# Routed expert outputs weighted at PSUM and added into two sums in DRAM, with all gate and up weights on chip

## The chip, the cores and the metric

The kernel runs on one core of a Trainium2 chip. Times are device microseconds of one launch, in timed runs without a profile. The kernel before was timed three times; its median is 205.45 us.

## What is computed

Eight sequences of 128 tokens with 256 channels (1024 tokens, float32) go through two blocks. The first is a WKV recurrence over time, with keys from the layer norm of `x` and values from the context, and its result is added to `x`. The second is a mixture of experts: 32 experts, 4 picked for each token, no more than 256 rows kept for one expert. Cut to what matters:

```python
x = x + wkv(time_decay, time_first, layernorm(x), ctx)            # 8 x 128 x 256
h = rmsnorm(layernorm(x)) * norm_w
scores = softmax(h @ gate_w.T); topk_w, topk_ids = top_k(scores, 4); topk_w /= sum(topk_w)
buf[expert, pos] = h[token]                                       # E=32 experts, C=256 rows each
g, u = split(buf @ w13)                                           # w13: 32 x 256 x 256
eo = (silu(g) * u) @ w2                                           # w2:  32 x 128 x 256
routed[token] += eo[expert, pos] * topk_w                         # 4096 picks in all
out = x + layernorm(x) + routed + shared_expert(h)
```

## The kernel before

The work is written by hand for each engine: every engine has its own program, and semaphores order them. SP (SyncE) issues nearly all plain DMAs, POOL issues all indirect ones. A queue issues in the order of its program, so what stands behind a waiting instruction waits too. The kernel has three stages.

**Routing stage** (the `run([...])` lists). Eight sequences pass through a software pipeline on PE, DVE, ACT and POOL. For each sequence `b` it ends with the picks of 128 tokens: `slot_all[:, b, k]` is the row of the DRAM table `rows_in` (32 experts, `ROWS_E` = 1024 rows each) into which pick `k` of a token goes. `n_row[:, b, :]` is the normalised token with 8 tag columns behind it (the four expert numbers, then the four numbers of the picks), which ACT copies from `tags` (L459). POOL issues four indirect DMAs a sequence (`scatter`, L318), 32 in all, each writing 128 rows of 264 floats. Meanwhile SP issues (L192 to L227) the inputs, 32 DMAs of zeros into the first 256 rows of every expert in `rows_in` (L204; unused rows must be zero), the weights `w13` of the first four experts (L210) and all of `w2` (L227, four DMAs of 1 MB). At the end DVE adds the shared expert's output to `base_all` (L682).

**Expert stage.** For expert `e` SP loads its 256 rows into one of `WB` = 4 buffers `xg` (L214). PE transposes them (`rows_to_channels`, L874), ACT copies them from PSUM to SBUF (L476), PE multiplies with gate and up weights (`gate_up_half`, L882), ACT takes silu (L481), DVE multiplies (L730), PE multiplies with `w2` (`down_half`, L899), DVE copies the 256 output rows from PSUM into `yo` (L737). The second half of the 256 rows is computed only where an expert has over 128 rows (`pe.If`). POOL scatters the output with two indirect DMAs of 128 rows each into `rows_out` (`scatter_out`, L333), a DRAM table with one row for each of the 4096 picks. Where a row goes is worked out by DVE from the tags (L718, L722, L724); unused rows get a number outside the table and are left out. PE's order is transposes of `e + 1`, gate and up of `e`, down of `e - 1`. `w13` of later experts is loaded four experts ahead (L210). `yo`, `xg`, `w13b` and `pick_idx` all have four buffers, so DVE waits for the scatter of expert `e - 4` (`row_out`) before it works out the rows of expert `e`. SP also stores the last output row of every expert (`store_last`, L221) for an overflow case that this data doesn't take. On ACT, DVE, POOL and SP the middle experts run in a loop of four experts an iteration (`Fori`).

**Last stage.** SP waits for all scatters, loads the four picks of every token (`G`, nine DMAs, 4 MB, L265), and DVE (five sequences, L769) or ACT and POOL (three sequences, L503 and L372) weight them with `w_all` and add them to `base_all`. Eight DMAs write the result.

The scatter that the change touches:

```python
def scatter_out(e, q):
    pool.wait_ge(s["pick_ready"], e + 1)
    pool.wait_ge(s["f_yo"], e + 1)
    for a in range(2):
        pool.indirect_dma_start(rows_out, bass.IndirectOffsetOnAxis(ap=pick_idx[:, q, a:a + 1], axis=0),
                                yo[:, q, a, :], None, bounds_check=PICKS - 1, oob_is_err=False)\
            .then_inc(row_out[q], 16)
```

Of the kernel before, what the change touches and what calls it, by code (L numbers as in the profile page):

```python
# [4 lines left out]
F32 = mybir.dt.float32  # L5
BF16 = mybir.dt.bfloat16
I32 = mybir.dt.int32
# [5 lines left out]
P = 128  # L13
# [7 lines left out]
PICKS = B * T * K  # L21
RW = C + 2 * K
OUTSIDE = 16384
U_MAX = 60.0
POOL_SUMS = (1, 3, 6)
FIRST = 2
W2L = 4
SHARED_AFTER = 5
WB = 4


def xattn_moe(nc, x, ctx_in, time_decay, time_first, norm_w, gate_w, w13, w2, sh_gate, sh_up, sh_down, out):
    ctx = ExitStack()
    with ctx:
# [3 lines left out]
        def sem(name):  # L38
# [4 lines left out]
        rows_out = nc.dram_tensor("rows_out", (PICKS, C), F32, kind="Internal").ap()  # L43
# [6 lines left out]
        w_all = sb("w_all", [P, B, K])  # L50
        slot_all = sb("slot_all", [P, B, K], I32)
        tags = sb("tags", [P, B, 2 * K])
# [4 lines left out]
        big = sb("big", [P, E], I32)  # L57
# [24 lines left out]
        zeros = sb("zeros", [P, 4 * RW])  # L82
# [32 lines left out]
        ew = sb("ew", [P, B, K])  # L115
        esum = sb("esum", [P, B])
        rsum = sb("rsum", [P, B])
# [5 lines left out]
        late_row = sb("late_row", [P, C])  # L123

        w13b = [sb(f"w13b{q}", [P, HC, 2, F]) for q in range(WB)]
        w2_all = sb("w2_all", [P, E, C])
        xg = [sb(f"xg{q}", [P, 2, RW]) for q in range(WB)]
        own = sb("own", [P, WB, 2, K])
        owned = sb("owned", [P, WB, 2])
        pick_idx = sb("pick_idx", [P, WB, 2], I32)  # L130
        xT = sb("xT", [P, 2, HC, CAP])
        sg = sb("sg", [P, 2, CAP])
        act_t = sb("act_t", [P, 2, CAP])
        sg_all = sb("sg_all", [P, B, T])
        yo = sb("yo", [P, WB, 2, C])
        G = sb("G", [P, B, K, C])
        res = sb("res", [P, B, C])
        part = sb("part", [P, 2, K - 1, C])
        pool_part = sb("pool_part", [P, K - 1, C])
# [15 lines left out]
        names = """held_pool colT_ready cols6_done x0_in x1_in v0_in v1_in col_in gw_in sh_in sdn_in zero_set consts ident_set tri_set  # L155
# [3 lines left out]
            top_ready idx_done expert_ready nmax_done ew_ready rsum_done w_done tagged onehot_done mask_ready  # L159
            pos_ready slots_done picked_done slot_ready own_done owned_done pick_ready fits_done last_all_done last_set slot_max_done slot_top_done overflow_done fixed pickno_ready  # L160
            gu_ready gu_done sh_s sh_a tot_ready big_done beyond_done sh_y sh_b f_xt f_x f_g f_s f_a f_y f_yo tail_part res_ready weighted pool_part_done pool_res_ready""".split()
        s = {n: sem(n) for n in names}
        scattered = [sem(f"scattered{b}") for b in range(B)]
        w_in = [sem(f"w_in{q}") for q in range(WB)]
        w2_in = [sem(f"w2_in{g}") for g in range(W2L)]
        xg_in = [sem(f"xg_in{q}") for q in range(WB)]
        row_out = [sem(f"row_out{q}") for q in range(WB)]
        gathered = [sem(f"gathered{b}") for b in range(B + 1)]
        last_stored = [sem(f"last_stored{q}") for q in range(WB)]
# [4 lines left out]
        pool_out_done = sem("pool_out_done")  # L174
# [13 lines left out]
        def _(sp):  # L188
# [10 lines left out]

            sp.wait_ge(s["zero_set"], 1)  # L200
            zv = rows_in.rearrange("(e n) c -> n e c", n=ROWS_E)
            for a in range(2):
                for e in range(0, E, 2):
                    sp.dma_start(zv[a * P:(a + 1) * P, e:e + 2, :],  # L204
                                 zeros[:, 0:2 * RW].rearrange("p (e c) -> p e c", e=2)).then_inc(zeroed[a], 16)

            sp.dma_start(sdn[:, :], sh_down).then_inc(s["sdn_in"], 16)

            def load_weights(e, q):
                sp.dma_start(w13b[q][:, :, :, :].rearrange("p h a f -> p h (a f)"),  # L210
                             w13[bass.ds(e, 1)].rearrange("o (h p) f -> p (o h) f", p=P)).then_inc(w_in[q], 16)

            def load_rows(e, q):
                sp.dma_start(xg[q][:, :, :],  # L214
                             rows_in[bass.ds(e * ROWS_E, CAP), :].rearrange("(a p) c -> p a c", p=P))\
                    .then_inc(xg_in[q], 16)

            def store_last(e, q):

                sp.wait_ge(s["f_yo"], e + 1)  # L220
                sp.dma_start(last_rows[bass.ds(e, 1), :], yo[P - 1:P, q, 1, :]).then_inc(last_stored[q], 16)  # L221
# [725 lines left out]
```

## Time and profile before

| | us |
|---|---|
| timed runs, median of 3 | 205.45 |
| timed runs, lowest and highest | 204.16 to 205.67 |
| span of the one profiled execution | 228.0 |
| busy in that span: PE, DVE, POOL, ACT | 139.5, 120.4, 115.6, 84.8 |
| chain that ended last, largest shares | PE 36%, issue 20%, SP queue 19% |

The profile is one execution, which took longer than the timed ones. The page gives busy times of each engine, the span in 40 slices of 5.7 us (busy tenths, the TensorE clock in tenths, GB/s of the DMA engines), and groups of instructions by source line. The chain of waits goes back from the last instruction, at each step to what released it. The timeline lists instructions in order of time, with the idle time before each one in brackets.

### The profile page before, as it was taken

The page shows a single profiled execution, that of the slowest core. Times are in us where ns is not written, and L with a number is a line of the kernel's source. Part 1 is how long each engine was busy: PE and PEld are TensorE (multiplying, and loading weights), DVE is VectorE, ACT ScalarE, POOL GpSimd, SP SyncE. Part 2 cuts the span into 40 slices and gives each one's busy share as a digit, 9 for nine tenths or more (in the row PEclk, how much of TensorE's full clock was granted, in tenths as well). Part 3 has the DMA queues.
Part 4 walks back from the last instruction along what each step waited for, and adds up shares of the span by engine and source line. Part 5 has one row for each costly group of instructions (what it writes and reads, how often), then busy time and mean ns, then how long its engine had stood idle before and what let it go on. Part 6 is the DMA issues. An engine that isn't in the chain of part 4 may idle for free.

```text
span 228.0 us, 3659 instructions
## 1 busy us (share of the span) xinstructions
PE 139.5 (61%) x819; PEld 119.8 (53%) x819; DVE 120.4 (53%) x385; ACT 84.8 (37%) x254; POOL 115.6 (51%) x140
## 2 busy tenths in 40 slices
PE   1124887787774879969895948858499479200000
PEld 0112765676663559959794837837398377100000
DVE  2878999997433344555253531536237055303990
ACT  3165678566563024434214231335225032002410
POOL 6201156888877500754563736555464646632740
PEclk9999996555555799988999788999979958755555
DMA  5999999998222264775775657465665731129930
GB/s 173 334 340 340 338 339 364 365 373 301 96 99 95 95 198 134 235 204 153 218 198 176 192 161 220 136 189 158 185 172 171 232 115 52 43 69 359 385 122 23
DMA packets 40270, 46.46 MB, mean 204 GB/s; under 512 B 4585, under 2 KB 37045, under 8 KB 40252
## 3 DMA queue, kind: packets, MB, share of 16 engines
q1 hardware_dynamic: 35200, 37.30, 53.2%
q0 software_dynamic: 4608, 8.54, 10.5%
q10 hardware_dynamic: 444, 0.40, 0.5%
q8 instruction: 9, 0.15, 0.2%
q14 instruction: 9, 0.07, 0.1%
HBM read 27.95 MB, written 22.45 MB: 221 GB/s over the span
## 4 chain that ended last, share of the span: by engine, by line
PE 36%; issue 20%; SPq 19%; another core or an unknown queue 7%; DVE 7%; DMA 5%; ACT 2%; POOL 0%; POOLq 0%; ACTq 0%; DVEq 0%
PE bank L882 18%; PE bank L899 11%; SPq L204 10%; PE bank L874 8%; SPq L227 5%; DVE part L769 4%; DMA G<-rows_out 3%; DVE act_t L730 1%; ACT xT L476 1%; DMA xg<-rows_in 1%; ACT sg L481 1%; DVE res L769 1%; SPq L210 1%; DMA rows_out<-yo,pick_idx 1%
## 5 line engine op out<-in xcount | busy, mean ns | idle before, releaser
L333 POOL DMA_INDIRECT rows_out<-yo,pick_idx x64 | 62.6, 978 | 55.7 <-issue 47.8
L882 PE MATMUL bank<-xT,w13b 128*128 128x128 f32 x368 | 51.6, 294 | 8.5 <-issue 5.6
L882 PEld LDWEIGHTS bank<-xT,w13b 128*128 128x128 f32 x368 | 48.1, 208 | 11.0 <-issue 11.0
L476 ACT ACTIVATE xT<-bank,cols 128x256 f32<-128x256 f32 x64 | 26.8, 473 | 43.0 <-PE bank L874 37.0
L899 PE MATMUL bank<-w_all,act_t 128*128 128x256 f32 x92 | 29.7, 434 | 16.0 <-DVE act_t L730 14.9
L730 DVE TENSOR_TENSOR act_t<-sg,bank 128x256 f32<-128x256 f32 x32 | 13.5, 421 | 49.3 <-ACT sg L481 36.5
L318 POOL DMA_INDIRECT rows_in<-n_row,slot_all x32 | 32.5, 1015 | 10.0 <-issue 10.0
L481 ACT ACTIVATE sg<-bank 128x256 f32<-128x256 f32 x32 | 12.3, 386 | 44.6 <-PE bank L882 25.1
L899 PEld LDWEIGHTS bank<-w_all,act_t 128*128 128x128 f32 x92 | 16.5, 209 | 18.8 <-issue 17.9
L737 DVE COPY yo<-bank 128x512 f32<-128x512 f32 x32 | 22.0, 687 | 6.6 <-remote 3.3
L874 PE MATMUL bank<-ident,xg 128*128 128x128 f32 x128 | 22.0, 301 | 1.3 <-DMA xg<-rows_in 1.2
L874 PEld LDWEIGHTS bank<-ident,xg 128*128 128x128 f32 x128 | 18.0, 157 | 6.2 <-issue 2.7
L839 PE MATMUL bank<-hT,sgu 128*128 128x128 f32 x64 | 16.1, 432 | 0.0
L308 POOL TENSOR_TENSOR rs<-ve,neg_half 128x2 f32<-128x2 f32 x8 | 5.9, 736 | 17.4 <-DVE ve L624 17.3
L839 PEld LDWEIGHTS bank<-hT,sgu 128*128 128x128 f32 x64 | 14.3, 326 | 0.0
L503 ACT ACTIVATE G<-G,w_all 128x256 f32<-128x256 f32 x12 | 5.1, 496 | 17.1 <-DMA G<-rows_out 17.1
L810 PE MATMUL bank<-ident,n_row 128*128 128x128 f32 x16 | 5.3, 430 | 9.6 <-ACT n_row L431 9.6
L718 DVE SCALAR_TENSOR_TENSOR own<-xg,iota_e 128x8 f32<-128x8 f32 x32 | 7.0, 219 | 7.4 <-issue 4.4
L562 DVE TENSOR_TENSOR_SCAN S<-decay,bank 128x512 f32<-128x512 f32 x8 | 9.7, 1209 | 1.1 <-PE bank L794 1.1
L769 DVE SCALAR_TENSOR_TENSOR part<-G,w_all,base_all 128x256 f32<-128x256 f32 x5 | 3.8, 767 | 10.4 <-DMA G<-rows_out 10.4
L794 PE MATMUL bank<-ident,ek 128*128 128x128 f32 x16 | 5.1, 420 | 6.4 <-DVE ekv L556 6.3
L819 PE MATMUL bank<-gwT,hT 128*128 128x32 f32 x32 | 7.5, 374 | 1.8 <-ACT hT L444 1.8
(109 smaller groups left out, 194.3 us busy)
## 6 DMA issues: line engine op xcount, KB each, us to landing
rows_in<-zeros SPq DMA_DIRECT2D x32, 264.0 KB, 6.4
xg<-rows_in SPq DMA_DIRECT2D x32, 264.0 KB
w13b<-in_L_ffn_w_dram SPq DMA_DIRECT2D x32, 256.0 KB
w_all<-in_L_ffn_w_dram SPq DMA_DIRECT2D x4, 1024.0 KB
G<-rows_out SPq DMA_DIRECT2D x7, 512.0 KB, 7.1
rows_out<-yo,pick_idx POOLq DMA_INDIRECT x64
x_all<-in_x_dram SPq DMA_DIRECT2D x1, 768.0 KB, 5.2
v_all<-in_ctx_dram SPq DMA_DIRECT2D x1, 768.0 KB, 7.6
```

Source lines behind the costliest of these rows:

```text
L204: sp.dma_start(zv[a * P:(a + 1) * P, e:e + 2, :], zeros[:, 0:2 * RW].rearrange("p (e c) -> p e c", e=2)).then_inc(zeroed[a], 16)
L318: pool.indirect_dma_start(rows_in, bass.IndirectOffsetOnAxis(ap=slot_all[:, b, k:k + 1], axis=0), n_row[:, b, :], None)\
L333: pool.indirect_dma_start(rows_out, bass.IndirectOffsetOnAxis(ap=pick_idx[:, q, a:a + 1], axis=0), yo[:, q, a, :], None, bounds_check=PICK ...
L476: act.activation(xT[:, j, h, :], FX[j][:, h, :], ACT.Copy, scale=nw[:, h:h + 1]).then_inc(s["f_x"], 1)
L481: act.activation(sg[:, j, :], FG[j][:, 0, :], ACT.Silu).then_inc(s["f_s"], 1)
L730: dve.tensor_tensor(act_t[:, j, :], sg[:, j, :], FG[j][:, 1, :], ALU.mult).then_inc(s["f_a"], 1)
L737: dve.tensor_copy(yo[:, q, :, :], FY[q % 2]).then_inc(s["f_yo"], 1)
L769: dve.scalar_tensor_tensor(out=dst, in0=G[:, b, k, :], scalar=w_all[:, b, k:k + 1], in1=src, op0=ALU.mult, op1=ALU.add)\
L839: last = nc.tensor.matmul(SGU[:, a, :], sgu[:, h, a, :], hT[:, j, h, :], start=(h == 0), stop=(h == HC - 1))
L874: last = nc.tensor.transpose(FX[q % 2][:, h, a * P:(a + 1) * P], xg[q][:, a, h * P:(h + 1) * P], ident[:, :])
L882: last = nc.tensor.matmul(FG[q % 2][:, a, cols], w13b[q][:, h, a, :], xT[:, q % 2, h, cols], start=(h == 0), stop=(h == HC - 1))
L899: return nc.tensor.matmul(FY[q % 2][:, a, :], act_t[:, q % 2, a * P:(a + 1) * P], w2_all[:, bass.ds(e, 1), :].rearrange("p o c -> p (o c)" ...
```

## The change

It does these things together:

- **Weights.** All of `w13` gets its place in SBUF (`w13_all`, 64 KB a partition). SP loads it in eight DMAs of 1 MB between the four of `w2`, all ahead of the first row load. The loads of 256 KB within the expert stage are gone. `yo[e]` lies over `w13` of the same expert, once that is used, so each expert has its own output buffer.
- **Sums.** `rows_out` is replaced by `sums`: two tables of 1280 rows (256 spare rows, then the 1024 tokens). The tokens of the first table start as `base_all` (a store of 1 MB that SP issues after the first six row loads), the second table and the spare rows as zeros (1.5 MB, issued behind the weights). Expert `e` adds to table `e % 2`.
- **Scatter.** `scatter_out` uses `compute_op=ALU.add`: the DMA reads the rows in DRAM, adds, and writes them. Unused rows are added to the spare rows, so all 128 rows of each DMA are moved. As two additions to one row must not overlap, POOL waits for expert `e - 2` to have landed before it issues the scatter of `e`. The wait for `pick_ready` is gone.
- **Weighting.** A row of `rows_in` is two floats longer (266): expert numbers, the four exponentials, one over their sum, and the row in `sums`. DVE writes the expert numbers straight into `n_row`, ACT the exponentials, and DVE the reciprocal (`pick_norm`). DVE weights the output as it copies it from PSUM (two `tensor_scalar` of 256 columns instead of one copy of 512).
- **Order and buffers.** No `Fori` is left on any engine. `xg` has six buffers. DVE works out rows two experts ahead. Gate and up matmuls take 256 columns at once instead of 128 twice. The flags `second` are bits of two registers loaded once, instead of a load for each expert. ACT copies the last output rows (`last_to_sbuf`), and one DMA stores them all.
- **Last stage.** SP loads the two sums (eight DMAs, 2 MB), DVE adds them (four additions), and four DMAs write the result.

The core of the diff:

```diff
-            for q in range(WB):
-                load_weights(q, q)
+            for g in range(EARLY):
+                load_w13(g)
+                if g % 2 == 0:
+                    load_w2(g // 2)
+            sp.dma_start(sums[0:SPARE].rearrange("(p a) c -> p (a c)", a=2), zero_rows).then_inc(sums_zeroed, 16)
+            sp.dma_start(sums[ACC:2 * ACC].rearrange("(p n a) c -> p n (a c)", p=P, a=2),
+                         zero_rows.unsqueeze(1).to_broadcast([P, ACC // (2 * P), 2 * C])).then_inc(sums_zeroed, 16)
...
             for b in range(B):
                 sp.wait_ge(scattered[b], 16 * K)
+            for e in range(XB):
+                load_rows(e)
+            sp.wait_ge(s["sh_b"], B // 2)
+            sp.dma_start(sums[SPARE:ACC].rearrange("(b p) c -> p b c", p=P), base_all[:, :, :]).then_inc(base_stored, 16)
...
             def scatter_out(e, q):
-                pool.wait_ge(s["pick_ready"], e + 1)
                 pool.wait_ge(s["f_yo"], e + 1)
-                pool.sem_inc(s["held_pool"], 1)
+                if e >= ACCS:
+                    pool.wait_ge(row_out[(e - ACCS) % YB], 32 * ((e - ACCS) // YB + 1))
                 for a in range(2):
-                    pool.indirect_dma_start(rows_out, bass.IndirectOffsetOnAxis(ap=pick_idx[:, q, a:a + 1], axis=0),
-                                            yo[:, q, a, :], None, bounds_check=PICKS - 1, oob_is_err=False)\
-                        .then_inc(row_out[q], 16)
+                    pool.indirect_dma_start(sums, bass.IndirectOffsetOnAxis(ap=pick_idx[:, e, a:a + 1], axis=0),
+                                            yo[e][:, a, :], None, compute_op=ALU.add).then_inc(row_out[q], 16)
...
-                dve.tensor_copy(yo[:, q, :, :], FY[q % 2]).then_inc(s["f_yo"], 1)
+                for a in range(2):
+                    last = dve.tensor_scalar(yo[e][:, a, :], FY[e % 2][:, a, :], owned[:, e, a:a + 1],
+                                             xg[e % XB][:, a, NORM:NORM + 1], ALU.mult, ALU.mult)
+                last.then_inc(s["f_yo"], 1)
...
+            for c in range(B // 2):
+                dve.wait_ge(sum_in[c], 16 * ACCS)
+                dve.tensor_tensor(G[0][:, 2 * c:2 * c + 2, :], G[0][:, 2 * c:2 * c + 2, :], G[1][:, 2 * c:2 * c + 2, :],
+                                  ALU.add).then_inc(s["res_ready"], 1)
...
                 with pe.If(second != 0):
-                    for a in range(2):
-                        gate_up_half(q, a, slice(P, 2 * P))
-                for a in range(2):
-                    last = gate_up_half(q, a, slice(0, P))
-                last.then_inc(s["f_g"], 1)
+                    gate_up_slots(e, j, CAP)
+                with pe.Else():
+                    gate_up_slots(e, j, P)
```

## Rows read from the trace of the kernel before

**Rows 1.** The page: share of the chain, and the 40 slices for clock and DMA.

```profile
PE 36%; issue 20%; SPq 19%; another core or an unknown queue 7%; DVE 7%; DMA 5%; ACT 2%; POOL 0%; POOLq 0%; ACTq 0%; DVEq 0%
PEclk9999996555555799988999788999979958755555
GB/s 173 334 340 340 338 339 364 365 373 301 96 99 95 95 198 134 235 204 153 218 198 176 192 161 220 136 189 158 185 172 171 232 115 52 43 69 359 385 122 23
```

**Rows 2.** Stretches of time: busy us of each engine (instructions), clock, DMA share, GB/s.

```profile
32.00:54.00 22.00, 15.94 (x85) 13.27 (x83) 20.83 (x80) 16.38 (x63) 17.17 (x18) 0.59 1.08 366
54.00:79.00 25.00, 17.18 (x85) 14.13 (x86) 10.61 (x39) 9.63 (x32) 18.60 (x20) 0.54 0.32 116
98.00:198.00 100.00, 75.77 (x474) 66.39 (x474) 42.16 (x137) 30.43 (x79) 53.93 (x56) 0.89 0.57 167
```

**Rows 3.** The page's groups for indirect DMAs and expert matmuls.

```profile
L333 POOL DMA_INDIRECT rows_out<-yo,pick_idx x64 | 62.6, 978 | 55.7 <-issue 47.8
L882 PE MATMUL bank<-xT,w13b 128*128 128x128 f32 x368 | 51.6, 294 | 8.5 <-issue 5.6
L318 POOL DMA_INDIRECT rows_in<-n_row,slot_all x32 | 32.5, 1015 | 10.0 <-issue 10.0
```

**Rows 4.** Timeline of the expert stage: first output copy, then scatters on POOL.

```profile
89.04 0.69 DVE L737 COPY yo<-bank 128x512 f32<-128x512 f32 x1
90.64 1.20 POOL L333 DMA_INDIRECT rows_out<-yo,pick_idx  x1 [6.95 <-DVE pick_idx L724]
...
117.05 0.98 POOL L333 DMA_INDIRECT rows_out<-yo,pick_idx  x1 [0.31 <-issue]
118.33 0.98 POOL L333 DMA_INDIRECT rows_out<-yo,pick_idx  x1 [0.30 <-issue]
120.28 0.97 POOL L333 DMA_INDIRECT rows_out<-yo,pick_idx  x1 [0.97 <-issue]
121.56 0.97 POOL L333 DMA_INDIRECT rows_out<-yo,pick_idx  x1 [0.30 <-issue]
```

**Rows 5.** Timeline of PE over the first experts, outside any loop.

```profile
88.84 0.60 PE L874 MATMUL bank<-ident,xg 128*128 128x128 f32 x4
91.93 0.60 PE L874 MATMUL bank<-ident,xg 128*128 128x128 f32 x4
...
94.12 0.60 PE L874 MATMUL bank<-ident,xg 128*128 128x128 f32 x4
95.89 0.60 PE L874 MATMUL bank<-ident,xg 128*128 128x128 f32 x4
```

**Rows 6.** Chain of waits, pieces in order of time: start us, us, what.

```profile
79.17 2.78 DMA xg<-rows_in
82.08 0.64 PE bank L874 x4
...
86.35 1.79 PE bank L882 x16
88.14 0.87 PE bank L899 x4
...
176.79 5.72 another core or an unknown queue
...
200.99 2.30 DMA rows_out<-yo,pick_idx
203.44 0.35 SPq L265
...
222.11 0.48 DVE res L769
```

**Rows 7.** Timeline of the routing stage: first and last scatter, a sum of 512 columns.

```profile
31.48 1.31 POOL L318 DMA_INDIRECT rows_in<-n_row,slot_all  x1 [0.28 <-issue]
...
75.19 0.69 DVE L682 TENSOR_TENSOR base_all<-base_all,bank 128x512 f32<-128x512 f32 x1 [1.25 <-issue]
76.65 0.96 POOL L318 DMA_INDIRECT rows_in<-n_row,slot_all  x1 [0.30 <-issue]
```

**Rows 8.** Timeline of the last stage: the first gathered sequence is there.

```profile
206.78 0.48 DVE L769 SCALAR_TENSOR_TENSOR part<-G,w_all,base_all 128x256 f32<-128x256 f32 x1 [8.58 <-DMA G<-rows_out]
```

More of the change, by code:

```diff
@@ new lines, in _ @@
+            for e in range(E):
+                if e + XB < E:
+                    sp.wait_ge(s["f_xt"], e + 1)
+                    sp.wait_ge(s["f_yo"], e + 1)
+                    load_rows(e + XB)
+                if e % 2 == 0 and EARLY + e // 2 < W13L:
+                    load_w13(EARLY + e // 2)
+                    if (EARLY + e // 2) % 2 == 0:
+                        load_w2((EARLY + e // 2) // 2)
+            sp.wait_ge(s["f_raw"], E)
+            sp.dma_start(last_rows.rearrange("(o e) c -> o e c", o=1), w2_all[P - 1:P, :, :]).then_inc(last_stored, 16)
@@ L677, in _ @@
             dve.wait_ge(s["tot_ready"], 1)
-            dve.tensor_scalar(big[:, :], TOT, CAP / 2 + 0.5, None, ALU.is_gt).then_inc(s["big_done"], 1)
+            dve.wait_ge(s["bit_set"], 5)
+            dve.scalar_tensor_tensor(out=halves[:, :], in0=TOT, scalar=CAP / 2 + 0.5, in1=bit[:, :], op0=ALU.is_gt,
+                                     op1=ALU.mult).then_inc(s["halves_done"], 1)
+            dve.wait_ge(s["halves_done"], 1)
+            with nc.allow_low_precision("sums of different powers of two below 2^16"):
+                dve.tensor_reduce(big[:, :], halves[:, :].rearrange("p (g n) -> p g n", n=BITS), AX.X, ALU.add)\
+                    .then_inc(s["big_done"], 1)
             for c in range(B // 2):
@@ L753, in _ @@
-            rows_out_to_sbuf(E - 1, WB - 1, E // WB - 1)
-            dve.wait_ge(s["sh_b"], B // 2)
-            dve.wait_ge(s["w_done"], 1)
-            mine = [b for b in range(B) if b not in POOL_SUMS]
-            for n, b in enumerate(mine):
-                dve.wait_ge(gathered[b], 16)
-                for k in range(K):
-                    src = base_all[:, b, :] if k == 0 else part[:, n % 2, k - 1, :]
-                    dst = res[:, b, :] if k == K - 1 else part[:, n % 2, k, :]
-                    if k:
-                        dve.wait_ge(s["tail_part"], (K - 1) * n + k)
-                    if b == B - 1 and k == K // 2:
-                        dve.wait_ge(gathered[B], 16)
-                    dve.scalar_tensor_tensor(out=dst, in0=G[:, b, k, :], scalar=w_all[:, b, k:k + 1], in1=src,
-                                             op0=ALU.mult, op1=ALU.add)\
-                        .then_inc(s["res_ready" if k == K - 1 else "tail_part"], 1)
+                    rows_out_to_sbuf(e - 1)
@@ L903, in down @@
+            def down(e, j, second):
+                if e % (E // W2L) == 0:
+                    pe.wait_ge(w2_in[e // (E // W2L)], 16)
                 pe.wait_ge(s["f_a"], e + 1)
[L904 to L905 removed]
                 with pe.If(second != 0):
[L907 to L911 removed]
```

353 lines of the change are left out of this document (156 added, 197 removed).

## The prediction

> **What bounds the kernel now.** I read the page first, then the chain of waits, then the timeline at each seam of the three stages. The chain's shares [rows 1] name PE (36%) and "issue" (20%), but an average over stages can't say what a change is worth, so I cut the span where the chain passes from one stage to the next [rows 6]: the first row load is released at 79.17 and PE starts on it at 82.08; the last scatter lands at 200.99 + 2.30 = 203.29; the last DVE sum ends at 222.59; the span ends at 228.0.
>
> The profiled span is 22.5 us above the timed median of 205.45. Part of that can be seen. The chain holds 7% (some 16 us) of "another core or an unknown queue" [rows 1], in pieces of up to 5.72 us in the middle of the expert stage, on a kernel with one core [rows 6]. I take these stalls, and the half clock that follows them, as belonging to the profiled execution. So I build a sum for the expert stage that doesn't hold them, and test it on the median.
>
> Two engines could pace that stage. **PE**: outside the loops it runs without a gap. One expert with over 128 rows takes 91.93 - 88.84 = 3.09 us, one with fewer 95.89 - 94.12 = 1.77 us [rows 5]. The 368 gate and up records [rows 3] are 8 for each of 32 experts and 8 more for each large one, so (368 - 256) / 8 = 14 are large. 14 x 3.09 + 18 x 1.77 = 75.1 us. **POOL**: one scatter takes 0.98 us and the next starts 0.30 us later, 1.28 us in all, so 2.56 us an expert; at a loop's end the gap is 0.97 instead of 0.30 [rows 4]. 32 x 2.56 = 82 us, and 8 loop ends at 0.67 add 5.4. So POOL needs more than PE, and with four buffers DVE and PE are held to it.
>
> The sum for before: first PE work 82.1; first scatter at 90.64, 8.6 later; 31 further experts at 2.56 make 79.4; seven loop ends 4.7; second scatter and landing 1.28 + 2.30 = 3.6; last stage 228.0 - 203.3 = 24.7. That is 203.1, 2.4 below the median. The sum holds well enough to go on: POOL's instruction rate, not PE, sets the expert stage in timed runs.
>
> **The change part by part.**
>
> *Weights and zeros ahead of the expert stage.* DMA is full (366 GB/s, share 1.08) to the slice that ends at 57 us, where it is 301 GB/s, then 96 [rows 1, 2]; I put the end of the queue at 55.5. Added to it: 28 x 256 KB of `w13` (7.34 MB), zeroing 1.57 MB, and 0.07 MB for longer zero rows, together 8.98 MB. The 32 scatters of the routing stage go on to 78.7 at 116 GB/s (2.7 MB from 55.5) [rows 2, 7]. (8.98 + 2.7) MB at 366 GB/s is 32 us, so the queue is empty at about 87.5. The row loads stand behind the weights in the same queue. Before, 2.9 us lie between the release and PE's start [rows 6]; now the load is issued before the queue is empty, so I add only 0.5 us: PE starts at 88.0, +5.9. Bounds: 0, if the weights got through beside the scatters, and +9 with the whole 2.9 behind 88. The routing stage itself stays as long: POOL is nearly without a gap from 31.48 to 77.6 [rows 7] and gets no DMA more; ACT's copy of tags goes, a reciprocal on DVE comes.
>
> *`base_all` store.* 1.05 MB behind six row loads (1.6 MB): 2.7 / 0.366 = 7.3 us after 87.5, so 95 and some landing time, against a first scatter at 88.0 + 8.6 = 96.6. Hidden by about 1 us; if not, it costs that.
>
> *Loops unrolled, flags loaded once, larger matmuls.* POOL loses its loop ends: -4.7. Matmuls of 256 columns take 0.87 / 4 = 0.217 us each, of 128 columns 1.79 / 16 = 0.112 [rows 6]: 8 of the one equal 16 of the other, so PE gains nothing here. DVE's second instruction at the output costs 0.3 us an expert on an engine busy 42 of 100 us [rows 2]; ACT's copy of the last rows is as small. Both lie beside POOL's pace. Without that cover they would have 2.35 us of PE an expert above them still.
>
> *No weight loads in the stage.* They lie beside POOL's work; nothing gained on the path. The scatter reads as well as writes now, and moves all 256 rows instead of 128 on average. Per expert 272 KB of rows, 262 KB read, 262 KB written: even if all three count, 0.8 MB at 366 GB/s is 2.2 us. Below POOL's pace, but no longer far below (167 GB/s before [rows 2]).
>
> *The new wait.* It stands on POOL, with all later scatters behind it, and for these only the last stage waits: every expert has its own output buffer, so PE and DVE run ahead. One table's cycle takes two experts: scatter, second scatter 1.28 later, landing 2.30 after its start [rows 6], plus x for the addition, plus the time from a semaphore to the start of the scatter, 90.64 - 89.73 = 0.9 us [rows 4]. Together 4.5 + x, against 2 x 2.56 = 5.12 of POOL's own. The wait is free up to x = 0.6; beyond, every us of x costs 15.5 us over the stage and 1 us at its end.
>
> The trace shows no accumulating DMA, so x is bounded. From below 0: nothing makes an addition land sooner than a plain write. From above a whole second transfer, 2.78 us like the row load [rows 6]. Between them: the first gathered sequence (512 KB) is used 206.78 - 203.44 = 3.34 us after its issue [rows 6, 8], of which 1.43 are bytes at 366 GB/s and 1.9 fixed for issue, read trip and receipt. The accumulating scatter already pays issue and receipt. A third of 1.9 for the read trip and 131 KB / 366 GB/s = 0.36 for the bytes give x = 1.0, which I take. The cycle is then 5.5, 2.75 an expert.
>
> That an addition reads as much again is also what the Trainium skill says ("Collectives: The Full Stack", "The bandwidth ceiling"): it needs two source reads. No row here shows it.
>
> *Is the instruction itself longer?* The two kinds of indirect DMA in the trace take 0.98 and 1.02 us in spite of different rows and targets [rows 3], so I take the same; with half as much again (0.5) it would be 64 x 0.5 = 32 us, less what the wait already costs (6): +26.
>
> *Last stage.* 2.1 MB instead of 4.2: 1.9 fixed + 5.7 of bytes + 0.1 to the first issue = 7.7. The last of four sums, 0.69 [rows 7]. From the last DVE end to the end of the span 228.0 - 222.6 = 5.4 as before, and 0.3 for an output DMA twice as large. Together 14.1 against 24.7: -10.6.
>
> **The sum.** 88.0 + 8.6 + 31 x 2.75 (85.3) + 1.28 + 2.30 + 1.0 + 14.1 = 200.6. The same sum for before was 2.4 too low, for waits between PE and POOL that a compute side running ahead mostly removes; I add 0.9: **201.5 us**, against 205.45.
>
> **The rivals.**
>
> *The wait is free* (x up to 0.6). Then 31 x 2.56 and x = 0.6: 88.0 + 8.6 + 79.4 + 4.2 + 14.1 + 0.9 = 195. For it: 1 KB rows are moved by 16 engines that stand at 57% in the stage [rows 2]. Against: now they must read first.
>
> *Landing decides, the other way* (slower). The place is the new wait. From x = 1.4 on the gain of the last stage is used up: 201.5 + 16.5 x 0.4 = 208. At x = 2 it is 218, at 2.78 it is 231. For it: under load a landing may be longer than the 2.30 read in a quiet moment at the end, and the row loads now share the engines with twice the scatter bytes. Against: the engines aren't full.
>
> The Trainium skill speaks for this one ("DMA: Bandwidth & Descriptors", "Latency and other measured facts"): HBM access takes 0.2 us on average and 2 us at high load. With an added read at the loaded figure x would be over 2 and the time about 220; with the other it would be the free wait. The trace has no row for a read under load within a scatter.
>
> *The instruction is longer*: 201.5 + 26 = 227, as above. Against it: both forms cost the same today.
>
> *The weights don't delay the start*, or the change there does nothing: 196 with x = 1.0. For it: reads of weights and writes of zeros may overlap better than the 366 GB/s. Against: DMA share 1.08.
>
> **How the numbers follow.** Forecast (x from 0.6 to 1.2, or 1.0 with the start where it was) 0.40; free wait 0.20; landing decides 0.30, of which a quarter within 1%; longer instruction 0.10. About 1% is what a measurement of this kernel can tell from no change: under 203.4 is faster, over 207.5 slower. The forecast's own range, 195 to 206, holds a sixth within 1%. So faster 0.33 + 0.20 = 0.53, same 0.07 + 0.07 = 0.14, slower 0.33. The range goes from 191 (free wait and an early start) to 222 (x = 2.2); above it are the rest of the landing rival and most of the longer instruction, about 1 in 8.
>
> **What would show it.** In the profile after: scatters on POOL about 2.75 us apart by expert, with gaps that end with a DMA landing; PE finished well before the last scatter; PE's first expert work near 88 with 366 GB/s up to there; the last stage near 14 us. Scatters 2.56 apart with gaps of 0.30 mean the free wait; pairs with gaps of over 1.5 us mean that landing decides; a mean above 1.2 us for the scatter means the instruction. If PE instead ends last, the reading that POOL sets the pace is wrong, and if the timed median differs from this sum while its steps are right, the stalls that I left out are in timed runs too.

## The result, and the profile after

| | before | after |
|---|---|---|
| timed, median of 4 runs (us) | 204.81 | 250.19 |
| lowest to highest | 203.62 to 205.67 | 248.59 to 251.89 |
| span of the profiled execution | 228.0 | 246.9 |

The kernel after takes 1.221 times as long as the kernel before, 95% interval 1.210 to 1.231. The prediction was 201.5 us, faster.

One thing about the measure itself comes out of the experiments and is needed to read them: beside the later kernels, on five other occasions, the kernel before took 232 to 237 us, while the kernel after, run again on one of them, took 249.2, nearly as at first. There the ratio is 1.058 (1.048 to 1.069). Each kernel below is compared with the runs of before that stand beside it. Where runs of one kernel lie apart, medians are of those within 1.5% of its fastest, while the expectations quote medians of all runs (222.3, 211.8, 238). Ratios with an interval are estimates over the same runs, and can differ from the ratio of two medians by half a per cent.

The page of after: the groups of the two indirect DMAs and of the weighting, then the 40 slices of 6.2 us. They answer to [rows 1, 3].

```profile
L342 POOL DMA_INDIRECT sums<-w_all,pick_idx x64 | 99.4, 1553 | 33.2 <-issue 16.6
L327 POOL DMA_INDIRECT rows_in<-n_row,slot_all x32 | 32.0, 1001 | 16.4 <-issue 15.5
L723 DVE TENSOR_SCALAR w_all<-bank,owned,xg 128x256 f32<-128x256 f32 x64 | 31.7, 537 | 0.6 <-PE bank L865 0.4
...
PEclk9999999955555569599999999999985555555555
GB/s 182 311 236 229 242 234 229 239 307 374 391 393 391 390 394 293 287 149 140 194 188 160 174 173 205 179 207 174 102 83 65 70 78 65 71 78 65 65 237 273
```

The adding scatter takes 1.55 us of POOL, the plain one took 0.98 [rows 3]. And from 12 to 49 us the DMA engines move 230 to 240 GB/s where the kernel before had 340 to 370 [rows 1]. The timeline of POOL in after shows where time goes at the start and in the expert stage, against [rows 4, 7]:

```profile
2.09 0.10 POOL L285 MEMSET var_add<- 128x1 f32 x1
11.31 0.16 POOL L286 IOTA iota_e<- 128x32 f32 x1 [9.12 <-issue]
...
54.02 1.11 POOL L327 DMA_INDIRECT rows_in<-n_row,slot_all  x1 [7.47 <-issue]
...
91.72 0.96 POOL L327 DMA_INDIRECT rows_in<-n_row,slot_all  x1 [0.30 <-issue]
98.69 0.38 POOL L335 PARTITION_ALL_REDUCE slot_top<-slot_max  x1 [6.01 <-issue]
110.81 1.80 POOL L342 DMA_INDIRECT sums<-w_all,pick_idx  x1 [11.73 <-DVE w_all L723]
...
114.76 1.55 POOL L342 DMA_INDIRECT sums<-w_all,pick_idx  x1 [0.30 <-issue]
116.61 1.54 POOL L342 DMA_INDIRECT sums<-w_all,pick_idx  x1 [0.30 <-issue]
119.55 1.54 POOL L342 DMA_INDIRECT sums<-w_all,pick_idx  x1 [1.39 <-DMA sums<-w_all,pick_idx]
...
230.15 1.55 POOL L342 DMA_INDIRECT sums<-w_all,pick_idx  x1 [0.30 <-issue]
```

POOL sits idle for 9 us before its first iota (an instruction that fills a tile with counted-up numbers). The routing scatters of the second sequence start at 54.0, and the last routing scatter at 91.7 instead of 76.7 [rows 7]. Then 64 adding scatters go out from 110.8 to 230.2, nearly always 0.30 us apart. The chain of waits in after at the two ends of the expert stage (start us, us, what), against [rows 6]:

```profile
91.72 5.87 DMA rows_in<-n_row,slot_all
...
97.67 2.81 DMA xg<-rows_in
...
100.53 1.13 PE bank L842 x4
...
230.15 3.61 DMA sums<-w_all,pick_idx
...
237.40 6.16 DMA v_all<-sums
243.58 0.69 DVE x_all L740
```

| step of the sum | predicted | after | difference |
|---|---|---|---|
| PE's first expert work | 88.0 | 100.53 | +12.5 |
| from there to the first scatter | 8.6 | 10.28 | +1.7 |
| first to last scatter (31 x 2.75 + 1.28) | 86.5 | 119.34 | +32.8 |
| last landing | 3.30 | 3.61 | +0.3 |
| last stage | 14.1 | 13.1 | -1.0 |
| allowance | 0.9 | - | -0.9 |
| span | 201.5 | 246.9 | +45.4 |

### The profile page after: what moved, and what is told of

Its sections match the earlier page's. It is cut to its first block, busy times and chain, and to the rows that moved or that the text cites. A ratio compares the mean times of both kernels' runs of the same rounds, so it can differ in the third digit from the quotient of the medians.

```text
span 246.9 us, 2751 instructions
## 1 busy us (share of the span) xinstructions
PE 126.7 (51%) x707; PEld 108.9 (44%) x707; DVE 115.3 (47%) x409; ACT 92.5 (37%) x266; POOL 144.1 (58%) x134
## 4 chain that ended last, share of the span: by engine, by line
PE 25%; DMA 22%; POOL 19%; SPq 16%; issue 14%; DVE 1%; POOLq 1%; ACT 1%; ACTq 0%
PE bank L851 14%; SPq L223 13%; DMA sums<-w_all,pick_idx 10%; POOL rows_in L327 9%; POOL sums L342 8%; PE bank L865 6%; PE bank L842 5%; DMA rows_in<-xT 4%; DMA xg<-rows_in 3%; DMA v_all<-sums 2%; DMA rows_in<-n_row,slot_all 2%; SPq L267 1%; POOL rs L316 1%; DVE w_all L723 1%; POOLq L41 1%
## 5 line engine op out<-in xcount | busy, mean ns | idle before, releaser
L342 POOL DMA_INDIRECT sums<-w_all,pick_idx x64 | 99.4, 1553 | 33.2 <-issue 16.6
L851 PE MATMUL bank<-xT,w_all 128*128 128x128 f32 (+1 forms) x256 | 46.6, 326 | 0.5 <-ACT xT L472 0.5
L851 PEld LDWEIGHTS bank<-xT,w_all 128*128 128x128 f32 x256 | 38.4, 194 | 3.4 <-issue 0.9
L723 DVE TENSOR_SCALAR w_all<-bank,owned,xg 128x256 f32<-128x256 f32 x64 | 31.7, 537 | 0.6 <-PE bank L865 0.4
L740 DVE TENSOR_TENSOR x_all<-x_all,v_all 128x512 f32<-128x512 f32 x4 | 2.8, 692 | 59.1 <-DMA v_all<-sums 59.1
L865 PE MATMUL bank<-w_all,act_t 128*128 128x256 f32 x92 | 25.7, 386 | 1.6 <-DVE act_t L717 1.3
L842 PE MATMUL bank<-ident,xg 128*128 128x128 f32 x128 | 20.1, 283 | 6.5 <-DMA xg<-rows_in 6.4
L842 PEld LDWEIGHTS bank<-ident,xg 128*128 128x128 f32 x128 | 16.3, 146 | 10.8 <-DMA xg<-rows_in 8.1
L482 ACT ACTIVATE w_all<-bank 32x256 f32<-32x256 f32 x32 | 12.1, 377 | 10.5 <-DVE w_all L723 9.8
L780 PEld LDWEIGHTS bank<-ident,n_row 128*128 128x128 f32 x16 | 2.2, 196 | 17.8 <-ACT n_row L432 17.8
## 6 DMA issues: line engine op xcount, KB each, us to landing
sums<-xT SPq DMA_DIRECT2D x1, 1280.0 KB, 11.5
```

The source lines that it names most:

```text
L342: pool.indirect_dma_start(sums, bass.IndirectOffsetOnAxis(ap=pick_idx[:, e, a:a + 1], axis=0), yo[e][:, a, :], None, compute_op=ALU.add).t ...
L482: act.activation(raw[e][P - 32:P, :], FY[e % 2][P - 32:P, 1, :], ACT.Copy).then_inc(s["f_raw"], 1)
L723: last = dve.tensor_scalar(yo[e][:, a, :], FY[e % 2][:, a, :], owned[:, e, a:a + 1], xg[e % XB][:, a, NORM:NORM + 1], ALU.mult, ALU.mult)
L842: last = nc.tensor.transpose(FX[j][:, h, a * P:(a + 1) * P], xg[e % XB][:, a, h * P:(h + 1) * P], ident[:, :])
L851: last = nc.tensor.matmul(FG[j][:, a, 0:slots], w13_all[:, e, h, a, :], xT[:, j, h, 0:slots], start=(h == 0), stop=(h == HC - 1))
L865: return nc.tensor.matmul(FY[j][:, a, :], act_t[:, j, a * P:(a + 1) * P], w2_all[:, e, :], start=True, stop=True)
```

## The experiments

### The row length and the adding form, one at a time

`a_rows272` is after with rows of 1088 bytes instead of 1064, the extra floats zero. `a_plain` is after with plain writes:

```diff
-RW = C + 2 * K + 2
+RW = 272
```
```diff
-                        yo[e][:, a, :], None, compute_op=ALU.add).then_inc(row_out[q], 16)
+                        yo[e][:, a, :], None).then_inc(row_out[q], 16)
```

> The changed kernel with rows of 272 floats (1088 bytes) instead of 266 (1064 bytes) in rows_in; six of them are zeros that nothing reads. Theory 'odd row length': DMA moves rows of 1064 bytes at 230 to 240 GB/s and rows of 1088 bytes at the 338 GB/s that 1056 bytes had before, so the zeros are done near 39 us instead of 54, and the first expert matmul starts near 88 instead of 100.5; the time falls by 10 to 14 us, to 236 to 240. Rival 'more bytes, late POOL': the start is late because of 9 MB more in the queue and of POOL's late first instructions; then 250 stays (2% more bytes, +1 us) and GB/s in the first 50 us stays below 250.

> The changed kernel with plain writes instead of additions in the 64 scatters to sums (the sums are left out, only the last writer stays); all waits stay. Theory 'the instruction': an accumulating DMA_INDIRECT keeps POOL for 1.55 us, a plain one for 0.98, so the pace falls from 1.85 to 1.28 us a scatter and the time by 63 x 0.57 = 36 us, to about 214. Rival 'landing': the wait for the scatter two experts back paces the stage; then gaps before the scatters stay over 0.3 us and the fall is what landing loses (3.7 to 2.3 us a cycle of two experts, 16 x 1.4 = 22 us), to about 228.

`b_rows266` is before with two more floats in a row (1064 bytes). `a_64rows` is after with each adding scatter cut to its first 64 rows (half of the rows are left out).

> The kernel before with rows of 266 floats (1064 bytes) instead of 264 (1056 bytes), nothing else. Theory 'odd row length': the zeros end some 15 us later, and so does the whole chain behind them: 218 to 221 us against 205. Rival 'more bytes': 0.8% more bytes in these DMAs, under 0.5 us: 205.

> The changed kernel with each accumulating scatter cut to its first 64 rows (the other 64 outputs are left out). If POOL's time is per row, the instruction falls from 1.55 to 0.8 to 1.0 us and the time by 35 to 45 us; if it is a fixed price of the addition, it stays at 1.5 and the time at 250. If landing paced the stage, it would fall by less than 10 us.

Measured, beside 233.3 for before on that occasion: `a_rows272` 244.6 (ratio 1.049, 1.042 to 1.057); `b_rows266` 250.9 (1.076, 1.063 to 1.089). Stretches of time, busy us of each engine, clock, DMA share, GB/s; first `a_rows272`:

```profile
8.00:32.00 24.00, 5.93 (x23) 4.07 (x24) 14.83 (x46) 9.39 (x31) 5.35 (x16) 1.00 1.11 344
32.00:54.00 22.00, 17.32 (x84) 14.56 (x82) 21.57 (x82) 15.63 (x58) 12.81 (x14) 0.69 1.09 360
```

then `b_rows266`:

```profile
8.00:32.00 24.00, 11.80 (x50) 9.19 (x49) 21.05 (x64) 12.72 (x40) 3.53 (x5) 1.00 1.11 236
32.00:54.00 22.00, 11.23 (x52) 9.57 (x51) 14.88 (x56) 9.02 (x35) 5.30 (x6) 1.00 1.11 209
```

Eight bytes more in a row bring the zeroing from 337 to 236 GB/s, at a DMA share that is full either way, and cost 17.6 us in time. 24 bytes more on top of those give the rate back. In the kernel after the same mend is worth 5.6 us of time (250.2 to 244.6), half of the 10 to 14 that I expected. A later kernel, `e_brows268` (before with 1072 bytes), took 244.0 beside 231.9 (1.052, 1.043 to 1.061) at 276 GB/s, between the two:

> The kernel before with rows of 268 floats, 1072 bytes (16 x 67; 1056 is 32 x 33, 1088 is 64 x 17, 1064 is 8 x 133). It shows what about 1064 bytes makes the zeroing slow. If any row that isn't a multiple of 32 bytes is slow: 215 to 250 GB/s in the first 50 us and 15 to 18 us more than before. If a multiple of 16 is enough: 340 GB/s and the time of before.

`a_plain` took 231.3 in its profiled run and 258.3 in its only other one, so its time rests on a single run. `a_64rows` took 242.1 (one run). Their scatters, first in `a_plain`, then in `a_64rows`:

```profile
L342 POOL DMA_INDIRECT sums<-w_all,pick_idx x64 | 61.8, 966 | 46.9 <-DVE w_all L723 23.8
L342 POOL DMA_INDIRECT sums<-w_all,pick_idx x64 | 90.0, 1406 | 30.6 <-issue 15.3 <-DVE w_all L723 11.9 <-DMA sums<-w_all,pick_idx 3.4
```

The plain form takes 966 ns, so the 0.59 us more belong to the adding form. Half the rows take off only 0.15 us of 1.55, so most of the price doesn't grow with the rows; 63 x 0.15 = 9 us is also about what the time fell by (8). Neither expectation was met in full: the instruction became shorter in `a_plain` as the theory has it, but the time fell by 19 us and not 36. The landings aren't the reason, for POOL waits for them only 3.0 us. It now waits 23.8 us for DVE, half of it inside the stage, and the first and the last scatter lie 96.0 us apart instead of 63 x 1.28 = 80.6.

### Both undone, and what is left

> The kernel after with both suspected causes undone: rows of `rows_in` of 1088 bytes instead of 1064, and the 64 scatters of the expert stage as plain writes (so the output leaves out the additions: each token keeps one expert's rows only). My theory: these two are all that the prediction missed, so the time comes near the prediction's sum with its own start corrected: PE starts at about 92, first scatter at 104, then 31 x 2.56 + 1.28 + 2.30 + 13.1 = 200.5. Rival: without the slow scatters another bound appears that the sum never held (in the run with plain writes alone the 32 experts took 96 us from first to last scatter, 3.1 each, with POOL waiting 24 us for DVE): 104 + 96 + 3.6 + 13 = 217, and the stage between first and last scatter is over 90 us.

219.8 us (all four runs: 218.8 to 225.6) beside 234.8. My theory fell, and the rival's 217 was near. So the adding form costs the kernel with 1088 bytes 25 us (244.6 to 219.8). Two more things are in the difference to 200.5: a late start (PE at 98.8 in the profile) and a long expert stage. In this stage there are times of 2 to 5 us in which PE, ACT and DVE stand still and POOL goes on; I call them holes. ACT in `a_272_plain`:

```profile
143.99 0.38 ACT L479 ACTIVATE sg<-bank 128x256 f32<-128x256 f32 x1
148.12 0.84 ACT L474 ACTIVATE xT<-bank,cols 128x256 f32<-128x256 f32 x2 [3.75 <-remote]
```

The kernel after has no such hole on PE once the stage is under way. The transposes from first to last (the tile view of `xg`: ns of one, first and last start) in after, then in `a_272_plain`, show it:

```profile
L842 PE MATMUL bank<-ident,xg x128: 272/273/472, 100.5 to 175.1; 128*128 128x128 f32 x128
```
```profile
L844 PE MATMUL bank<-ident,xg x128: 272/273/421, 98.8 to 193.2; 128*128 128x128 f32 x128
```

74.6 us against 94.4, and 107.4 in the kernel before (82.1 to 189.5). `f_no_add` below, the same program but for a branch that doesn't run, has 94.8. The routing stage, whose scatters are plain in every kernel, can have such holes too. DVE in `a_272_plain`:

```profile
83.33 0.19 DVE L643 TENSOR_TENSOR slots<-bank,slot 128x32 f32<-128x32 f32 x1 [3.74 <-remote]
88.37 0.19 DVE L670 SCALAR_TENSOR_TENSOR halves<-bank,bit 128x32 f32<-128x32 f32 x1 [3.01 <-remote]
```

There they explain the late start: PE begins the experts when the delayed shared expert is done, not when the rows are there. Two kernels on the base of `a_272_plain` ask what makes the holes. `d_paced` puts a fill on POOL behind each scatter, `d_late` holds all scatters until the last expert:

```diff
+                    pool.wait_ge(s["padded"], 2 * e + a)
+                    pool.memset(Y[:, :, :, :].rearrange("p j h t -> p (j h t)"), 0.0).then_inc(s["padded"], 1)
```
```diff
             pool.wait_ge(base_stored, 16)
+            pool.wait_ge(s["f_yo"], E)
```

> The kernel after with rows of 1088 bytes and plain scatters (additions left out), and behind each scatter a fill of 512 columns on POOL (0.54 us by the row of the first fill), so that POOL's cycle is that of the accumulating scatter, about 1.85 us, while the transfers stay plain. If the stalls of PE, ACT and DVE (2 to 5 us each, none with accumulating scatters, eleven on DVE with plain ones) come from the pace at which POOL issues, or from POOL waiting for them, they are gone: PE's transposes take about 74 us from first to last and the time is near 243. If the kind of the transfer makes them, they stay: 94 us from first to last.

> The kernel after with rows of 1088 bytes and plain scatters (additions left out), all scatters held until the last expert is computed. Nothing of POOL lies beside the compute engines then. If the scatters cause the stalls, PE needs 74 us from first to last transpose, as beside accumulating scatters, and the end is start 92 + 74 + 6 + 64 x 1.28 (82) + 2.3 + 13 = 269 to 272. If the stalls have another cause, the transposes take 94 us and the time is about 290.

`d_late` took 273.8, `d_paced` 228.6 and 234.0 in its two runs (beside 236.7). Transposes in `d_paced`, then in `d_late`:

```profile
L846 PE MATMUL bank<-ident,xg x128: 272/273/421, 98.8 to 172.8; 128*128 128x128 f32 x128
```
```profile
L845 PE MATMUL bank<-ident,xg x128: 272/273/332, 95.4 to 169.3; 128*128 128x128 f32 x128
```

74 us in both. So the holes of this stage need plain scatters beside the compute engines: they are gone when all scatters come later, and also when POOL is slowed, though the transfers are the same. POOL's cycle in `d_paced` is 1.67 us, not the 1.85 I expected, which takes 63 x 0.18 = 11 us off the 243:

```profile
134.89 0.97 POOL L344 DMA_INDIRECT sums<-w_all,pick_idx  x1 [0.16 <-issue]
135.86 0.54 POOL L347 MEMSET Y<- 128x512 f32 x1
136.56 0.97 POOL L344 DMA_INDIRECT sums<-w_all,pick_idx  x1 [0.17 <-issue]
```

That the adding scatter is free of the holes because it is slow itself (1.85 us) fits this, and isn't tested apart from its being another kind of transfer.

### Fewer scatters

`c_skip` (after, 1088 bytes) and `b_skip` (before, with POOL's and DVE's loops unrolled) leave out the second scatter of the 18 experts with at most 128 rows, which moves no token; the list is written in for these inputs. `b_unroll` is before with POOL's loop unrolled and nothing else.

```diff
-                for a in range(2):
+                for a in range(2 if e in LARGE else 1):
```

> The kernel after with rows of 1088 bytes and without the second scatter of the 18 experts that have at most 128 rows (their second half holds no token; which experts these are is written into the kernel for these inputs). 46 accumulating scatters instead of 64. If each costs POOL 1.85 us whatever it carries, and POOL paces the stage: 18 x 1.85 = 33 us less than the 244.6 of the 1088-byte kernel, less a few us that the wait for the table's last landing now takes (two small experts need 3.7 us of POOL, their landing over 4): 213 to 220. If the additions are limited by the rows they move (the skipped ones move rows to spare places), likewise. If the bound were PE or DVE, nothing: about 244. If the wait decided, it would show as gaps of over 1.5 us that end with a landing before most scatters, and the time would stay over 225.

> The kernel before without the second scatter of the 18 experts that have at most 128 rows, POOL's and DVE's expert loops unrolled for it. 46 plain scatters of 1.28 us are 59 us of POOL instead of 82. If POOL's instruction rate sets the expert stage of before, as the prediction had it, PE's 75 us become the bound and the ratio is 0.95 to 0.97 (7 to 12 us less). If the stage of before is set by the stalls between PE, ACT and DVE that its profile shows (16 us of unknown queues), it gains nothing: ratio 0.99 to 1.01.

> The kernel before with POOL's loop over the experts unrolled, nothing else. With the loop and all 64 scatters it took 238 us beside the kernel without the 18 empty scatters (unrolled on POOL and DVE), which took 212. If the 26 us come from the empty scatters (18 x 1.28 = 23 us of POOL), the unrolling alone gives the 4.7 us of the loop ends at most: ratio 0.98 to 1.0. If they come from the loops, the ratio is near 0.9.

`c_skip` 223.8 and `b_skip` 211.3, beside 234.8; `b_unroll` 235.4 beside 236.7 (0.998, 0.992 to 1.004). So 18 adding scatters fewer are worth some 21 us, less than the 33 of POOL's time, and the time is 4 us over the range I expected (213 to 220). The wait for the table now takes part of it: POOL's idle time that ends with a landing is 20.0 us in `c_skip`, 6.2 in `a_rows272`. In the kernel before, POOL's loop costs nothing that can be measured, and 18 plain scatters fewer (with DVE's loop unrolled) give 23 us, against 7 to 12 expected. That equals the 18 x 1.28 = 23 of POOL's time, but isn't simply that time, for POOL has 53 us of idle time before the scatters in `b_skip`. Part of the holes went: the transposes take from 85.3 to 175.7 instead of 84.9 to 193.3 in `b_unroll`.

`e_bskip_paced` adds to `b_skip` the fill of `d_paced`, 256 columns wide:

> The kernel before without the 18 empty second scatters (211.8 us), and behind each scatter a fill of 256 columns on POOL (about 0.3 us and a semaphore), so one scatter costs POOL about 1.65 us instead of 1.28. If the pace of plain scatters makes the stalls of PE, ACT and DVE, they go as they went in the after-type kernel with paced scatters: PE's transposes from first to last take 76 to 80 us instead of 90, and the time is 200 to 205. If pace matters only where POOL never waits (46 x 1.65 = 76 us is no more than PE's own 75), the stalls stay and the time is 211 to 214.

212.5 beside 231.9 (0.914, 0.906 to 0.922): nothing gained, transposes 83.3 to 171.9. With scatters 1.46 us apart at the closest, and POOL waiting 23.2 us for DVE (`pick_idx`), the holes stay. So whether the pace of the scatters or POOL's waiting behind the compute engines makes them isn't told apart.

### The wait

`c_tables4` is `a_rows272` with `ACCS = 4` and the zeroing of the two tables more.

> The kernel after with rows of 1088 bytes and four tables of sums instead of two, so each scatter waits for the landing of the one four experts back (the output leaves out the third and fourth table; zeroing grows by 2.6 MB at the end of the weights' queue). If the new wait costs nothing at two tables, the time stays within 3 us of the 244.6 of the same kernel with two; POOL's idle time that ends with a landing goes from 6.2 us to 0. If the wait is what costs, 10 us or more less.

243.7 against 244.6. POOL's idle time that ends with a landing goes from 6.2 to 1.2 us, and from first to last scatter it is 116.9 us instead of 122.7 (119.3 in after). The wait at two tables thus costs 2 to 6 us of the stage. The time hides it, because the first scatter came 4.6 us later here (108.3 against 103.7).

### POOL's idle time at the start

Every kernel derived from after has 7.6 to 12.2 us of idle time on POOL before its first iota, none derived from before has over 0.3, and the first routing scatter moves from 31.5 to 40. `e_fill` makes the fill ahead of it longer, `e_fill_skip` does so in `c_skip`; `f_no_add` is `a_272_plain` with the scatter in the overflow branch plain as well; `f_iota_first` is `c_skip` with the iotas ahead of the fills.

> The kernel after with rows of 1088 bytes, and the first fill on POOL over all 1024 columns of `xT` instead of 544, so that it takes about 0.95 us instead of 0.55 and POOL comes to its first iota about 0.45 us later (at 2.9 us instead of 2.2 to 2.5, as in the kernel before). Theory: POOL's 9 us of idle time before that iota, seen in every kernel derived from after and in none derived from before, hangs on reaching the iota too early; it goes, the first routing scatter starts at 31.5 instead of 40, PE starts at about 84 instead of 92, and the time is 236 instead of 244.6. Rival: the idle time has to do with something else in the changed program (its length, its other iotas); then nothing moves, first scatter at 40, time 244 to 245.

> The same longer first fill in the kernel with rows of 1088 bytes and without the 18 empty second scatters (223.8 us). If the early iota is what costs 9 us: 215 to 217. If not: 223 to 225. It also tells whether the changed kernel, mended in the three places found so far, beats the kernel before on chips where that takes 233 to 238, and whether it reaches the 205 of the first.

> The kernel with rows of 1088 bytes and plain scatters (222.3 us), in which now also the scatter of the overflow branch, which doesn't run with these inputs, is a plain write: no instruction of the program adds on the way any more (additions left out). Theory: POOL's 9 to 12 us of idle time before its first iota come with the adding form of the indirect DMA being in the program at all (every kernel derived from after has it, if only in that branch; none derived from before has). Then the first iota starts before 3 us, the first routing scatter at 31.5 instead of 41, PE's first expert work 8 to 10 us earlier and the time is 212 to 215. Rival: something else of the changed program; then the idle time stays at 9 to 12 us and the time at 219 to 226.

> The kernel after with rows of 1088 bytes and without the 18 empty second scatters (223.8 us), with POOL's four iotas ahead of its fills. If POOL's idle time hangs on what DMA does by then (reading and zeroing begin at 1 to 5 us), iotas at 0.8 us escape it and the time is 214 to 217. If whatever it waits for takes its 9 to 12 us from the start of the program, the wait only moves: it now stands ahead of the fill of the zeros too, the zeroing begins at 9 us or later, and the time is 224 to 235.

`e_fill` 245.6 (1.059, 1.049 to 1.069) and `e_fill_skip` 221.6 (0.953, 0.946 to 0.960), beside 231.9: the idle time stayed, 12.2 and 11.5 us. `f_no_add` 217.3 beside 232.1: it stayed as well (8.9), so the adding form isn't its cause. `f_iota_first` 218.6 beside 232.1 (0.945, 0.934 to 0.957), 5 us less than `c_skip`, and in the range of neither theory. POOL in `f_iota_first`:

```profile
8.12 0.16 POOL L282 IOTA iota_e<- 128x32 f32 x1 [7.62 <-issue]
...
38.51 1.31 POOL L334 DMA_INDIRECT rows_in<-n_row,slot_all  x1 [0.33 <-issue]
```

The wait moved with the iota, to 0.5 us, and is shorter ahead of the zeroing's traffic (7.6 us). So it stands ahead of this first iota wherever that is, with or without the adding form. The raw trace suggests why, and no run tested it. It holds instructions named `MODIFY_POOL_CONFIG` that the views leave out. In both kernels a pair of them stands ahead of the iota, and a second pair ahead of `partition_all_reduce` (the maximum over partitions that POOL takes at the end of the routing stage). The kernel before has a third pair, at 202.0, ahead of its sums on POOL (L372), which the change took away. If a launch starts with the configuration that the last one ended in, before already has the one that its iota needs, and after doesn't. All 20 traces fit: the 6 with a third pair have 0.3 us of idle time before the iota, the 14 without it 7.6 to 12.2. The change ahead of the all-reduce comes with 5.7 us of idle time in before; POOL in the kernel before:

```profile
2.92 0.17 POOL L285 IOTA iota_e<- 128x32 f32 x1 [0.28 <-issue]
...
83.31 0.38 POOL L326 PARTITION_ALL_REDUCE slot_top<-slot_max  x1 [5.70 <-issue]
```

The Trainium skill ("GPSIMD Engine Reference", "Instruction dispatch") has the first call of a freshly loaded kernel on this engine (there a kernel is the code of one kind of instruction) cost about 6 us, 5.95 measured. The 5.70 and 6.01 before the all-reduce agree; at the start it is 7.6 to 12.2.

### The kernel after, again

> The kernel after, unchanged, once more beside the kernel before. The kernel before took 205 us beside the first measurement of after, and 233 and 238 us beside later kernels. Theory: the 28 us are stalls in the expert stage of the kernel before, which comes and goes with the chip it is on; the kernel after, whose POOL is never ahead of the compute engines, doesn't have them and stays at 249 to 252, so the ratio here is 1.05 to 1.07. Rival: the whole chip is slower for every kernel, and after rises in proportion, to about 280, ratio 1.2.

249.2 beside 236.7. The kernel before moved between occasions; the kernel after, on the two on which it ran, didn't.

## Why the prediction was wrong

**"Is the instruction itself longer? ... so I take the same."** This step failed, and it is the largest term. The instruction takes 1.55 us instead of 0.98, so a scatter costs POOL 1.85 us instead of 1.28: 63 x 1.85 = 116.6 of the 119.3 us from first to last scatter, where the sum had 86.5. The mechanism was listed as a rival (+26 us at 0.5 more, chance 0.10), and the sign given for it, a mean above 1.2 us, came. I took two plain forms that cost the same as evidence for a third form that neither of them was. The rival's own price was near: 227, and with the 12.5 and 1.7 us of the start below it comes to 241 of the 247 in the profile. Taken by the runs, the adding form makes 25 (244.6 to 219.8) and the row length 5.6 (250.2 to 244.6) of the 48.7 us between 201.5 and 250.2. The adding form is worth less than 63 x 0.57 = 36 because the plain one wouldn't have reached its own pace: in `a_272_plain` the first and the last scatter lie 100.8 us apart, not 63 x 1.28 = 80.6. The remaining 18 us (201.5 to 219.8) lie in this shortfall and in the late start. So even if the adding form had cost the 0.98 us of the plain one, the forecast would have been too low.

**The landing, x = 1.0, and the new wait.** 3.61 us for the last landing, so x = 1.3. By the prediction's rule this would cost; but the longer instruction stretches POOL's two experts to 7.4 us, over the 1.85 + 3.61 + 0.9 = 6.4 of the table's cycle. The wait of the landing rival is there (3.2 us in all), off the scale of the result. It would bite with fewer scatters, as `c_skip` shows.

**PE's first work at 88.0.** 100.5, for other reasons than those given. "The routing stage itself stays as long" was wrong twice. POOL's first iota is 8.4 us late (11.31 against 2.92, cause inferred above); and the zeroing, which I priced by bytes (0.07 MB), loses 30% of its rate to rows of 1064 bytes. `a_rows272` tells these apart: with 1088 bytes PE starts at 92.0, so the late POOL and all else give 9.9, the row length 8.5 on top. These are single traces: PE starts at 91.5 to 98.8 in the ten kernels derived from after with 1088 bytes, and at 100.5 to 107.2 in the four with 1064. The two partly hide each other, as either delays the same scatters. The weights, for which I had taken all 5.9 us, show only in the landing of the last routing scatter, 5.87 us against 2.44 in `a_rows272`, where they are through by 85 us: 3.4 of the 8.5.

**First scatter 8.6 later.** 10.3: PE runs at the lower of its two clock levels there (granted clock 0.50 from 100 to 105 us, 1.00 from 82 to 87 in before), and four transposes take 1.13 us instead of 0.64 [rows 6].

**Right:** the last stage (13.1 for 14.1), PE finished long before the last scatter (175 against 230), no gain from wider matmuls, DVE's second instruction and ACT's copy hidden. The loop ends weren't worth the 4.7 us that the sum gave them (`b_unroll`).

**The stalls of the kernel before**, "as belonging to the profiled execution". This assumption failed too, though it didn't decide the sign. On five later occasions timed runs of before took 232 to 237, near its profile's span of 228. That the sum of 203.1 came within 2.4 us of the median was luck of the occasion: it left out holes that every trace of before or a kernel derived from it shows. The later runs were on chips 1, 14, 7, 4 and 1 again; chip 1 gave 233.3 and 232.1. The chip of the first occasion isn't on record, so whether chips differ or a chip changes stays open. That POOL alone sets the stage was also too simple: the holes are a third bound, and come with plain scatters beside the compute engines. What they are in the hardware, and why the first occasion is free of them, stays open. `d_paced` and `d_late` show what removes them in the kernel after, `e_bskip_paced` that the same remedy doesn't help before.

Of the kernels run, `b_skip`, the kernel before without its empty scatters, is the best: 211.3 us where before took 234.8. It wasn't run on an occasion where before takes 205. The kernel after, mended by row length, skipped scatters and order of the iotas (`f_iota_first`), gets to 0.945 of before where that takes 232, and doesn't reach `b_skip`. No mended kernel was seen below the 204.8 that before took on the first occasion.

## What to carry to other kernels

An operation that the trace doesn't show has no price there: bound it by the most that one like it could cost per instruction, and look first at the engine that is already the pace. Where a change alters the length of a row, cost the rate and not the bytes. And where it removes the last work of an engine, ask what state that work left behind for the next launch; here that is a guess that fits all traces, and not a tested cause.

## What the runs showed of the hardware

- An adding indirect DMA of 128 rows of 1 KB takes POOL 1.55 us, a plain one 0.97; with 64 rows the adding one takes 1.41. The last adding one lands 3.6 us after its start, the last plain one of before 2.3.
- Between 8 and 32 us, in which zeros are written to DRAM in rows of 1056, 1064, 1072 or 1088 bytes, the DMA engines moved 337, 236, 276 and 344 GB/s, with their share full in all four. Why is not shown.
- Ahead of POOL's `partition_all_reduce`, where its configuration is changed, POOL was idle for 5.70 us in before and 6.01 in after. Idle time of 7.6 to 12.2 us stood before its first iota in 14 kernels and 0.3 in 6; that this is the same cost is inferred.
- Plain scatters at 1.28 us apiece beside the compute engines came with holes of 2 to 5 us on PE, ACT and DVE (first to last transpose 94 us). With the scatters at 1.67 us apiece, or behind all compute, it was 74 us, in kernels derived from after.
